# Attention and experts on one core: output row numbers read from the token tiles, normalisation beside the expert tiles

## What is computed

```python
xn = layernorm(x)
S = einsum('hid,hjd->hij', K, Q) * SCALE        # 4 batches x 16 heads of 16, causal
C = softmax(where(delta < 0, -inf, S) + decay)  # decay = -(distance of the tokens)
s = (C @ V) @ o_w.T + o_b
probs = softmax(xn @ gate_w); the best 2 of 8 experts of each token, shares scaled by alpha
g = silu(sum over both of share * (gelu(xn @ fc1_w + fc1_b) @ fc2_w + fc2_b))
out = x + s * g
```

## Time and profile before

| what | before |
|---|---|
| median of 3 runs | 790.04 us (789.72 to 795.38) |
| the profiled execution | 788.32 us, span 786.4 us |
| PE busy | 726.5 us (92%) |
| PEld busy | 424.1 us (54%) |
| DVE busy | 564.4 us (72%) |
| ACT busy | 509.9 us (65%) |
| POOL busy | 245.4 us (31%) |

### The profile page before, as it was taken

The page is one execution under the profiler, slowest core; times in us unless marked ns, Lnnn a source line. Parts: engine busy times, 40 slices in busy tenths (PEclk is TensorE's granted clock), DMA queues, the critical chain, the costliest instruction groups (busy, mean ns, idle before and its releaser), DMA issues.

```text
span 786.4 us, 16602 instructions
## 1 busy us (share of the span) xinstructions
PE 726.5 (92%) x5194; PEld 424.1 (54%) x5195; DVE 564.4 (72%) x1532; ACT 509.9 (65%) x1044; POOL 245.4 (31%) x311
## 2 busy tenths in 40 slices
PE   4998998999999999999999999989989999999894
PEld 2554553444444444544444444434338899999663
DVE  2556989999989888888888889888304544444387
ACT  3775556567677676667667667557786666666354
POOL 0433222251123333223223222302143457454300
PEclk9999999999999999999999999999999999999998
DMA  8889945353566596577567568593556855555487
GB/s 200 243 214 269 243 148 125 39 102 90 105 134 121 119 147 126 115 143 150 112 121 165 105 112 164 89 163 84 123 95 179 209 181 159 167 162 165 154 289 246
DMA packets 85255, 119.49 MB, mean 152 GB/s; under 512 B 14175, under 2 KB 58719, under 8 KB 85119
## 3 DMA queue, kind: packets, MB, share of 16 engines
q1 hardware_dynamic: 76654, 94.50, 53.9%
q0 software_dynamic: 8528, 24.07, 10.3%
HBM read 72.61 MB, written 45.52 MB: 150 GB/s over the span
## 4 chain that ended last, share of the span: by engine, by line
PE 60%; DVE 12%; DMA 11%; issue 7%; ACT 5%; POOL 2%; SPq 2%; DVEq 0%; ACTq 0%; POOLq 0%
PE ps L1425 13%; PE ps L1362 13%; PE ps L1411 11%; PE ps L1513 8%; PE ps L1535 8%; DMA aug<-q_parts 5%; DVE mxa L1011 3%; DVE ps L1006 3%; ACT arena L890 3%; DMA arena<-y_dram 3%; PE ps L1414 2%; PE ps L1323 2%; PE ps L1496 2%; DMA q_parts<-arena 2%; POOL arena L659 2%
## 5 line engine op out<-in xcount | busy, mean ns | idle before, releaser
L890 ACT ACTIVATE arena<-ps 128x512 f32<-128x512 f32 x576 | 301.2, 613 | 146.9 <-PE ps L1414 130.4
L1362 PE MATMUL ps<-aug 105*128 105x512 bf16 (+3 forms) x768 | 218.7, 329 | 16.2 <-DVE mxa L1006 7.3
L1411 PE MATMUL ps<-aug 108*128 108x512 bf16 (+3 forms) x768 | 203.9, 326 | 4.8 <-ACT arena L890 2.7
L1011 DVE TENSOR_REDUCE mxa<-ps 128x1 f32<-128x512 f32 (+1 forms) x288 | 181.1, 683 | 19.4 <-PE ps L1362 15.3
L1425 PE MATMUL ps<-arena,v_q 128*32 128x512 f32 (+3 forms) x1536 | 140.4, 491 | 4.3 <-ACT arena L890 4.3
L1362 PEld LDWEIGHTS ps<-aug 105*128 105x128 bf16 x768 | 72.1, 97 | 125.3 <-DVE mxa L1006 39.2
L1006 DVE CUSTOM_DVE_ANT_0 ps<-ps,blank,mxa 128x256 f32<-128x256 f32 (+2 forms) x192 | 110.3, 621 | 27.2 <-PE ps L1362 26.9
L1414 PE MATMUL ps<-maskT_sb,idb 128*128 128x128 bf16 x512 | 112.4, 219 | 0.0
L1006 DVE CUSTOM_DVE_ANT_0 ps<-ps,blank 128x256 f32<-128x256 f32 (+2 forms) x192 | 100.9, 590 | 5.4 <-DVE mT L1031 2.8
L1411 PEld LDWEIGHTS ps<-aug 108*128 108x128 bf16 x768 | 71.4, 98 | 50.1 <-ACT arena L890 12.1
L775 POOL DMA_INDIRECT xs_dram<-arena,slot x64 | 62.8, 982 | 99.7 <-ACT arena L890 84.5
(11 more groups left out here) (139 smaller groups left out, 754.3 us busy)
## 6 DMA issues: line engine op xcount, KB each, us to landing
aug<-k_parts SPq DMA_DIRECT2D x96, 128.0 KB
aug<-q_parts SPq DMA_DIRECT2D x96, 128.0 KB
arena<-xs_dram SPq DMA_DIRECT2D x71, 128.0 KB
arena<-y_dram SPq DMA_DIRECT2D x16, 512.0 KB, 4.6
k_parts<-arena SPq DMA_DIRECT2D x16, 384.0 KB, 5.9
q_parts<-arena SPq DMA_DIRECT2D x16, 384.0 KB, 3.6
arena<-in_x SPq DMA_DIRECT2D x8, 512.0 KB, 5.8
xn_dram<-arena SPq DMA_DIRECT2D x8, 512.0 KB, 7.9
```

The costliest lines, as they stand in the source:

```text
L890: nc.scalar.activation(probs[SLOT[k, u]][:, half], score_bank(q, i), ACT.Exp).then_inc(exp_done, 1)
L1011: nc.vector.tensor_reduce(mxa[:, h:h + heads, col_], src, AX.X, ALU.max).then_inc(piece_used, 1)
L1362: ins = nc.tensor.matmul(out_, k_aug[n][0:SCORE_ROWS, h0 + h, ib * P:(ib + 1) * P], q_aug[n][0:SCORE_ROWS, h0 + h, lo:lo + width], start=T ...
L1411: ins = nc.tensor.matmul(out_, q_aug[n][0:ALL_ROWS, h, jb * P:(jb + 1) * P], k_aug[n][0:ALL_ROWS, h, i0:i0 + hi - lo], start=True, stop=lo ...
```

## The change

- The table load on POOL's queue (L783) goes. Instead a tile is loaded with all 257 columns, and DVE copies column 0 of each tile into `y_row_of` (`take_row`, 71 instructions of 128 x 1). `load_tile` additionally waits for that copy of the tile that held the buffer, and POOL's scatter for that of its own tile.
- The three inversions leave window 13 and stand on DVE between the two last evacuations.
- Store and loads of the inverses, and the loads of the numerators, leave windows 13 and 14; they stand on SP behind the stores of quad 14, those for batches 1, 2 and 3 among the tile loads (at n = 5, 18 and 31).
- POOL normalises batch 0 ahead of the first scatter, batches 1, 2 and 3 beside tiles 6 to 13, 18 to 25 and 32 to 39.
- SP's loop over tiles becomes straight code, with the loads of x behind chosen tiles.

```diff
-NORMALISE_BESIDE = range(24, 24 + A_PIECES)
+NORMALISE_BESIDE = {tile + n: (b, n) for b, tile in ((1, 6), (2, 18), (3, 32)) for n in range(A_PIECES)}
+X_PAIRS_BESIDE = (20, 21, 22, 23) + tuple(range(27, 71, CH)) + (SLOTS - 1,)
...
-        xg = [x_move[:, j, 0:D] for j in range(CH)]
+        xg = [x_move[:, j, 1:W] for j in range(CH)]
...
             load_sums(0, B - 1)
-            window(NQ - 3, (NQ - 3) % AUG, prepare_normalising)
-            load_a(1)
-            load_inverses(0, 1)
-            window(NQ - 2, (NQ - 2) % AUG)
-            load_a(2)
-            load_inverses(0, 2)
+            for q in range(FIRST_TAIL, NQ - 1):
+                window(q, q % AUG)
...
             def load_tile(n, j):
                 sp.wait_ge(t1_done, n + 1)
-                sp.dma_start(xg[j], xs_dram[bass.ts(n, P), 1:W]).then_inc(xg_in[j], 16)
+                if n >= CH:
+                    sp.wait_ge(row_taken, n - CH + 1)
+                sp.dma_start(x_move[:, j, :], xs_dram[bass.ts(n, P), :]).then_inc(xg_in[j], 16)
 
             for j in range(CH):
                 load_tile(j, j)
             window(NQ - 1, (NQ - 1) % AUG)
+            store_inverses(0, 0, B - 1)
+            sp.wait_ge(vq_ready, HQ * (B - 1) + 1)
+            load_a(0)
+            load_inverses(0, 0)
+            load_a(1)
+            load_a(2)
...
-            for n in range(CH, CH * straight):
+            pairs = iter(range(NT // 2))
+            for n in range(CH, SLOTS):
                 load_tile(n, n % CH)
-                if n == 6:
+                if n == 5:
+                    load_inverses(0, 1)
+                elif n == 6:
                     store_quad(NQ - 1)
...
-                elif n == 16:
+                elif n == 18:
+                    load_inverses(0, 2)
+                elif n == 31:
                     load_inverses(1, B - 1)
-                elif n >= CH * (straight - 1):
-                    if n == CH * (straight - 1):
+                if n in X_PAIRS_BESIDE:
+                    if n == X_PAIRS_BESIDE[0]:
                         sp.wait_ge(s_done, NU * NQ + 1)
-                    load_x_pair(n % CH)
...
-            pool.dma_start(y_row_of[:, :].bitcast(fp32), xs_t[:, 0:SLOTS, 0:1].rearrange("p n o -> p (n o)"),
-                           allow_slow_non_contiguous=True).then_inc(table_in, 16)
-            for b, q in enumerate(range(FIRST_TAIL, NQ)):
-                if q < NQ - 1:
-                    next_v(q, q % AUG)
-                for n in range(A_PIECES):
-                    normalise(b, n)
-            pool.wait_ge(table_in, 16)
+            for q in range(FIRST_TAIL, NQ - 1):
+                next_v(q, q % AUG)
+            for n in range(A_PIECES):
+                normalise(0, n)
 
             for n in range(SLOTS):
                 if n in NORMALISE_BESIDE:
-                    normalise(B - 1, n - NORMALISE_BESIDE[0])
+                    normalise(*NORMALISE_BESIDE[n])
+                pool.wait_ge(row_taken, n + 1)
                 pool.wait_ge(y_out, n + 3)
...
-            follow(NQ - 3, invert_first_sums(), INVERT_ITEM, every=6)
-            follow(NQ - 2)
-            for q in range(NQ - 2, NQ):
+            def evacuate(q):
                 dve.wait_ge(o_stored, 16 * 2 * HQ * (q + 1))
                 dve.wait_ge(pv_done, NTY * q + NTY + 3)
                 nc.vector.tensor_copy(oT, bank(6, 2)).then_inc(o_out, 1)
+
+            evacuate(NQ - 2)
+            dve.wait_ge(sums_in, 16)
+            for b in range(B - 1):
+                invert_sums(b)
+            evacuate(NQ - 1)
+
+            def take_row(n, j):
+                dve.wait_ge(xg_in[j % CH], 16 * rnd_of(n, j) + 16)
+                nc.vector.tensor_copy(y_row_of[:, bass.ds(n, 1)], x_move[:, j % CH, 0:1].bitcast(i32)).then_inc(row_taken, 1)
...
-            skewed(dve, ((h_evacuate, 2), (y_evacuate, 0)))
+            skewed(dve, ((take_row, 3), (h_evacuate, 2), (y_evacuate, 0)))
```

More of the change, by code:

```diff
@@ L78 @@
 STORE_AT = 6
-INVERT_ITEM = 4
 def masked_by_vector(piece):
@@ L109 @@
 PADS_STEP = 31
-NORMALISE_FROM = (NU * (NQ - 2), NU * (NQ - 1))
 SLOTS = (2 * B * T + E * (P - 1)) // P
@@ L382, in attention_moe_kernel @@
         rows_ready = sem("rows_ready"); x_moved = sem("x_moved"); scattered = sem("scattered")
-        table_in = sem("table_in")
+        row_taken = sem("row_taken")
         moe_w_in = sem("moe_w_in")
@@ L574, in _ @@
                                      src[:, per * t:per * (t + 1), :]).then_inc(moe_w_in, 16)
[L575 to L579, removed]
-            load_sums(0, B - 1)
-            window(NQ - 3, (NQ - 3) % AUG, prepare_normalising)
-            load_a(1)
-            load_inverses(0, 1)
-            window(NQ - 2, (NQ - 2) % AUG)
-            load_a(2)
-            load_inverses(0, 2)
+            load_sums(0, B - 1)
+            for q in range(FIRST_TAIL, NQ - 1):
+                window(q, q % AUG)
             sp.wait_ge(scattered, 16 * 2 * NT)
@@ L598, in _ @@
             window(NQ - 1, (NQ - 1) % AUG)
+            store_inverses(0, 0, B - 1)
[4 more added lines that the diff above has]
+            load_a(2)
             def load_x_pair(m):
                 sp.dma_start(x_all[:, bass.ts(m, 2), :], x_t[:, bass.ts(m, 2), :]).then_inc(x_all_in, 16)
-            rounds = SLOTS // CH
-            straight = rounds - (NT // 2 - CH - 1)
-            for n in range(CH, CH * straight):
+            pairs = iter(range(NT // 2))
+            for n in range(CH, SLOTS):
                 load_tile(n, n % CH)
-                if n == 6:
+                if n == 5:
+                    load_inverses(0, 1)
+                elif n == 6:
                     store_quad(NQ - 1)
@@ L615, in _ @@
                     store_inverses(1, B - 1, B)
-                elif n == 16:
+                elif n == 18:
+                    load_inverses(0, 2)
+                elif n == 31:
                     load_inverses(1, B - 1)
-                elif n >= CH * (straight - 1):
-                    if n == CH * (straight - 1):
+                if n in X_PAIRS_BESIDE:
+                    if n == X_PAIRS_BESIDE[0]:
                         sp.wait_ge(s_done, NU * NQ + 1)
-                    load_x_pair(n % CH)
[L622 to L628, removed]
+                    load_x_pair(next(pairs))
             def load_y(m, j):
@@ L747, in normalise @@
             def normalise(b, n):
-                if b < len(NORMALISE_FROM):
-                    pool.wait_ge(exp_done, NORMALISE_FROM[b] + 2 * n + SCORE_BANKS + 1)
                 if n == 0:
@@ L781, in _ @@
                 pool.wait_ge(scattered, 16 * 2 * (first_tile + count))
-            pool.wait_ge(xs_zero, 32 + 16 * E)
-            pool.dma_start(y_row_of[:, :].bitcast(fp32), xs_t[:, 0:SLOTS, 0:1].rearrange("p n o -> p (n o)"),
-                           allow_slow_non_contiguous=True).then_inc(table_in, 16)
-            for b, q in enumerate(range(FIRST_TAIL, NQ)):
-                if q < NQ - 1:
-                    next_v(q, q % AUG)
-                for n in range(A_PIECES):
-                    normalise(b, n)
-            pool.wait_ge(table_in, 16)
+            for q in range(FIRST_TAIL, NQ - 1):
+                next_v(q, q % AUG)
+            for n in range(A_PIECES):
+                normalise(0, n)
             for n in range(SLOTS):
                 if n in NORMALISE_BESIDE:
-                    normalise(B - 1, n - NORMALISE_BESIDE[0])
+                    normalise(*NORMALISE_BESIDE[n])
+                pool.wait_ge(row_taken, n + 1)
                 pool.wait_ge(y_out, n + 3)
@@ L1200, in follow @@
                     follow_item(q, first_item(q), i, item)
[L1202 to L1208, removed]
             follow(0, choose_experts(), ROUTE_FROM)
@@ L1212, in _ @@
             follow(2, place_tiles(), every=2)
-            for q in range(3, NQ - 3):
+            for q in range(3, NQ - 1):
                 follow(q)
-            follow(NQ - 3, invert_first_sums(), INVERT_ITEM, every=6)
-            follow(NQ - 2)
-            for q in range(NQ - 2, NQ):
+            def evacuate(q):
                 dve.wait_ge(o_stored, 16 * 2 * HQ * (q + 1))
```

## The result

The changed kernel takes 810.5 us (median of 4 runs, 808.3 to 811.53); the kernel before, run beside it, 791.37 us (4 runs, 789.72 to 795.38). The ratio is **1.0238 [1.02, 1.0276]**: slower, by 19 us, with the lower end of the interval right at 2%. The prediction had slower, by 13.4 us, and 795 to 809 us as its range: the median lies 1.5 us above it, the fastest of the four runs, which is the profiled one, inside it.

What follows compares the result with a forecast made beforehand. PE, busy for all 40.00 of 40 us in the expert stage, bounds the kernel. Terms -3.0 + 0.5 + 0.7 + 6.5 + 5.3 + 3.4 = +13.4 us give 801.7 profiled, 803.4 median; range 795 to 809 us.

Steps and rivals of the forecast that it cites:

- What bounds, and what is removed: PE bounds the expert stage; removing table load and inversions from window 13 takes 3.0 us off, bounds 2.4 and 3.6.
- What costs nothing: Inversions, take_row and added waits in the tile stage stay beside PE at 0; POOL's 16 more pieces cost 0.5 us.
- some tenths: Delay of a tile load by load_tile's added wait for take_row, of 8 us between its issue and use.
- tile 19's term: Behind batch 2's inverses, SP waits for POOL until 625.1; tile 19 lands at 634.3, wanted at 627.75: 6.5 us.
- The landing: A tile load queued behind eight inverse loads lands 9.0 us after their first issue, bounds 5.5 and 10.
- The clock: After two long PE pauses the granted clock falls, 1.7 us of work lost each: 3.4 us, bound below 0.
- the drift: In the tile stage, 16 more POOL pieces beside tiles, at 2.01 - 1.98 us each, cost 0.5 us.
- 1 (inverses come fast): Inverses run at 310 GB/s; tile loads land 6.4 us after first issue: +5.9 us, 796 us; chance 0.18.
- estimate of about 6 us: Skill's transfer formula, 2.3 us for 128 KB: inverses land about 6 us after first issue, sum near 796 us.
- 2 (POOL in time): a_normed is posted before SP needs it behind tile 18, so SP never stands still: 787.5 us; chance 0.07.
- 3 (batch 0 late): Store of the inverses takes 8.1 us, tile 6 is 5.3 late, third clock pause: 810 us; chance 0.10.
- 4 (no gain): Window 13's score rows are late for another reason, such as numerators: 3 us more, 806 on the forecast; chance 0.05.

Runs made afterwards that it cites:

- e9: Kernel before, without table load, row numbers copied from tiles four tiles ahead of DVE's second addition; inversions and normalising unmoved: 790.43 us, ratio 0.9979.
- e6: e4 with the table load kept and no row taken from the tiles: 792.84 us, ratio 1.0003 to the kernel before.
- e3: Kernel before, without table load, row numbers copied from tiles three tiles ahead; inversions, inverses and normalising unmoved: 792.41 us, ratio 0.9999.
- e1: The change with inverses of batches 2 and 3 behind tiles 22 and 40, pieces from tiles 24 and 40: 796.36 us, ratio 1.006.
- e2: The change with only one of the eight transfers of batch 2's inverses, SP's wait kept: 800.36 us, ratio 1.0112.
- e8: The change with POOL's batch 1 pieces beside tiles 4 to 11 in place of 6 to 13: 804.29 us, ratio 1.0157.
- e11: The change with every partition reading batch 2's inverses from its own DRAM row, same bytes and transfers: 809.02 us, ratio 1.0216.
- e12: The change with each batch's inverses read by two transfers writing 128 partitions, not eight writing 16: 821.75 us, ratio 1.0399.
- e13: e1 with the two wide inverse transfers per batch of e12: 811.98 us, ratio 1.028 to the kernel before.
- e4: The change with one inverse transfer behind each of eight tile loads per batch 1 to 3, POOL's pieces four tiles later: 788.72 us, ratio 0.9957.

## Why the prediction was right in kind and short in size

**What bounds, and what is removed.** Right: time lost by PE is the time lost, and window 13 gave 31.97 - 28.42 = 3.55 us, inside 2.4 to 3.6. How it divides is open. Without the table, with inversions and normalising left in place, the stretch is 29.50 us (e9): the table would be worth 2.5 us and the rest 1.1. With the table and without the others it is 33.63 (e6), more than before: the table would be worth all of it.

**What costs nothing.** The price was right (0.14 us a row, and from tile 20 to 31 the steps are as long as before: the shift stays at 8.65). The sentence that `load_tile`'s wait for `take_row` costs "some tenths" was wrong in one place, as e3 and e9 show: the order of DVE's list puts 3.2 us of bias work ahead of a row, and the row now holds SP. I had looked at DVE's idle time in an ordinary step, not at the one step with other work. In the change it cost less, since SP stands still behind tile 18 anyway.

The same bias work makes POOL late. Scatter 7 waits 3.24 us for it; the row is not the reason, as the same scatter waited in the kernel before:

```profile
613.82 0.97 POOL L796 DMA_INDIRECT y_dram<-arena,y_row_of  x1 [3.73 <-DVE arena L1262]
```

What is new is that a piece of normalising now stands behind each scatter. The two take 614.93 - 612.99 = 1.94 us of a step's 1.98, so POOL can make up hardly anything: it runs to scatter 13 with gaps of 0.17 us, and the last piece ends 624.48 - 618.73 = 5.75 us after the start of its step instead of 5.3. That step begins on PE with the transpose of tile 15:

```profile
618.73 0.38 PE L1484 MATMUL ps<-idf,arena 128*128 128x128 f32 x2
```

That is 0.45 of the 1.7 us by which tile 19's term was short. Of the 0.61 us up to tile 18 some 0.4 are a price that the prediction did not have: an addition of the bias work and one of POOL's pieces fall together, and the addition takes 0.83 us.

```profile
608.94 0.81 POOL L745 TENSOR_TENSOR v_all<-v_all,arena 128x256 f32<-128x256 f32 x1
```

```profile
609.21 0.83 DVE L1225 TENSOR_TENSOR arena<-ob_sb,arena 128x256 f32<-128x256 f32 x1
```

Before, without a piece beside it:

```profile
610.93 0.43 DVE L1237 TENSOR_TENSOR arena<-ob_sb,arena 128x256 f32<-128x256 f32 x1
```

It takes 0.83 us in all seven kernels that have a piece there (the change, e1, e2, e8, e11, e12, e13) and 0.42 to 0.43 in the six that do not. Why the two slow each other no run shows.

**The landing: the step that failed.** 9.0 us from the first inverse issue to a tile behind it was worked out from POOL's start at 9.67, less what POOL needs to start. But a tile behind the inverses must itself land after them; it should have been more than 9.67, not less. The trace of before had a closer bound: tile 17, queued behind the inverses of batch 3, was transposed without a wait 623.80 - 612.90 = 10.90 us after their first issue.

```profile
612.90 3.65 SPq L535 DMA_DIRECT2D arena<-inv_dram  x8
```

```profile
623.80 0.38 PE L1496 MATMUL ps<-idf,arena 128*128 128x128 f32 x2
```

Measured in the change: 10.69, 10.33 and 11.04 us; the upper bound, 10, was too low as well. Against the terms that is 1.5 us at tile 6 (its issue came as forecast: 586.78, forecast 591.0 less the gain of about 4), 1.3 at tile 19 and 1.1 at tile 32 (11.04 for 9.9; POOL's post there, 5.6 us after its step began, adds 0.3). Together 3.9 of the 5.2 us that the sum was short.

**The clock.** Two steps at half clock, +1.53 and +1.54: 3.1 for 3.4, right. Not foreseen was the end:

```profile
764.00:766.00 2.00, 0.00 (x0) 0.00 (x0) 1.62 (x5) 2.00 (x6) 0.00 (x0) 0.57 0.96 345
766.00:771.00 5.00, 4.91 (x12) 3.72 (x13) 5.00 (x11) 3.07 (x7) 0.00 (x0) 0.50 0.71 238
```

PE waits there 4.24 us, before 3.27, and the low level lasts from the pause to 771, for 4.91 us of work instead of 3.53: in all the end adds 1.0 us. Why the wait is longer no run shows.

**The sum.** It was 5.2 us short of the span: landing 3.9, POOL's post 0.8 (0.45 and 0.3), the end 1.0, the stretch to tile 18 0.6, the drift 0.3; less 1.0 of gain and 0.3 of clock. From the 803.4 us of the forecast to the median of 810.5 it is 7.1: of the other 1.9 us, 1.4 lie outside the span (3.3 us around it in the profiled execution, 1.9 before), which no row explains, and 0.5 comes from the medians, 2.2 us above the profiled execution where it was 1.7 before.

**The rivals.** 1 (inverses come fast) falls by the 10.3 us; how its 6.4 us follow from 310 GB/s the prediction does not show. The estimate of about 6 us is not borne out either. The Trainium skill, DMA: Bandwidth & Descriptors, "Anatomy of one DMA", gives the formula behind that estimate for transfers that GpSimd issues; these are SP's, so the runs do not test it. 2 (POOL in time) did not happen: SP waited until 624.55; e8, two tiles earlier, had a pause 4.2 us shorter. 3 (batch 0 late) fell: the store of the inverses, 8.1 us before, landed in 2.1 (KB, us from issue to landing):

```profile
inv_dram<-sums SPq DMA_DIRECT2D x1, 192.0 KB, 2.1
```

That the table load beside the store had made it slow explains only a part: without that load, in e3, it took 4.5. The rival's time, 810, was met by chance, by another road. 4 (no gain) fell by window 13.

## What to carry to other kernels

In these runs a block of transfers ahead of a paced load on the same queue cost its whole landing time, less the lead that the load had: nothing with 10.90 us of lead before the change, 8 us where a wait ahead of the block had used the lead up. Put one transfer behind each paced load, and the wait where its answer is already there: in e4 the same work then made PE wait for no tile. When a load is made to wait for a small instruction, look at what stands ahead of that instruction in the one step that is not like the others. And a list that has work for 1.94 of 1.98 us a step does not recover from one late step.

## What the runs showed of the hardware

- **Slow loads at full share.** The eight loads of the inverses move 137 GB/s before, and in the change, where those of batch 0 run alone, 144 GB/s, at a DMA share of 1.02; the numerators behind them in the same queue run at 410:

```profile
580.50:583.50 3.00, 2.10 (x24) 0.68 (x20) 0.00 (x0) 1.56 (x4) 3.00 (x5) 1.00 1.02 410
574.00:579.50 5.50, 4.41 (x46) 2.15 (x44) 0.00 (x0) 3.59 (x8) 0.00 (x0) 1.00 1.02 144
```

  The packets of both are of 4 KB; they take 464 ns on average between 574 and 579 us (172 packets) and 161 ns between 580.5 and 583.5 (296 packets). A row of its own for each partition (e11) does not help.
- **A load of one column slows what runs beside it.** 35.5 KB, 16.1 us, 67 GB/s for everything in that stretch together; without it the same stretch moves 117 GB/s at a share of 0.65.
- **Pauses of one length, two outcomes for the clock.** After 2.01 us before tile 6 the change stays at full clock; after 2.04 us at the same place in e1 PE worked at half (granted clock 1.00 and 0.50, the third figure from the end):

```profile
597.50:601.00 3.50, 3.50 (x26) 3.32 (x27) 1.35 (x5) 1.66 (x4) 0.28 (x1) 1.00 0.81 223
```

```profile
600.30:603.60 3.30, 3.30 (x14) 2.83 (x13) 0.96 (x3) 1.26 (x3) 0.00 (x0) 0.50 0.51 160
```

  So the price of a pause near 2 us was its length, or its length and about 1.5 us (the +1.53 and +1.54 of a step at half clock); in a sum it wants both ends.
- **An addition on DVE beside a multiplication on POOL.** Both are 128 x 256 in f32. Where they fall together, DVE takes 0.83 us for 0.43 and POOL 0.81 to 0.82 for 0.73 to 0.75, in seven kernels of seven.
